# An image pipeline written slot by slot: the transposes of a quarter step change places, the mean is taken off in another form, and slots move

## The reference, cut to what matters

```
h = concat(cls_tok, (relu(x @ W0.T) * (x @ W1.T)) @ Wo.T)
def bitlinear(x, w):                       # mean and variance over tokens AND features
    x = (x - mean(x, (1, 2))) * rsqrt(var(x, (1, 2)) + 1e-5)
    return act_quant(x) @ weight_quant(w).T   # round(x * 127 / max|x| of a token)
q, k, v = bitlinear(ln(h), w_q), ..., ...  # 16 heads of 16
h += bitlinear(softmax(q @ k.T / 4) @ v, w_o)
x2 = ln(h); top2 of softmax(x2 @ gate_w)   # router
h += sum over the 2 experts of p_e * (silu(x2 @ g_e) * (x2 @ u_e)) @ d_e
```

## Time and profile before

| | |
|---|---|
| median of three executions | 2512.09 us (2507.2 to 2514.85) |
| profiled execution, its own time | 2501.11 us |
| its span | 2499.2 us |
| mean granted TensorE clock | 0.934 |
| TensorE (PE) busy | 2160.9 us, 86% |
| VectorE (DVE) busy | 1521.1 us, 61% |
| ScalarE (ACT) busy | 1203.2 us, 48% |
| GpSimd (POOL) busy | 965.7 us, 39% |

### The profile page before, as it was taken

How to read it: one execution, slowest core, us unless ns; L and a number is a source line. 1 busy time by engine, 2 the same in 40 slices (tenths; PEclk the granted TensorE clock), 3 DMA queues, 4 the chain that set the end, 5 groups by cost and what they waited for, 6 DMA issues and landing times. The chain is left out here.

```text
span 2499.2 us, 46805 instructions
## 1 busy us (share of the span) xinstructions
PE 2160.9 (86%) x12048; PEld 1071.8 (43%) x12049; DVE 1521.1 (61%) x4004; ACT 1203.2 (48%) x2360; POOL 965.7 (39%) x894
## 2 busy tenths in 40 slices
PE   4889989899898998988989888984069999999998
PEld 2433434443433433443344333322036666666665
DVE  3477877777766786777777778763453333333332
ACT  1256656455554565555555556551233444444443
POOL 2323343342333433344343343232335555555554
PEclk9899999999998998999999999886589999999999
DMA  2322232222222222222222122201433333333332
GB/s 96 80 81 61 72 90 69 73 69 82 78 67 67 69 81 70 79 63 77 74 77 81 52 82 79 75 10 34 152 85 56 54 55 53 54 54 53 54 53 39
DMA packets 181070, 171.96 MB, mean 69 GB/s; under 512 B 40002, under 2 KB 169620, under 8 KB 180884
## 3 DMA queue, kind: packets, MB, share of 16 engines
q1 hardware_dynamic: 150612, 134.94, 18.1%
q0 software_dynamic: 30272, 34.80, 8.9%
HBM read 100.82 MB, written 68.93 MB: 68 GB/s over the span
## 5 line engine op out<-in xcount | busy, mean ns | idle before, releaser
L1141 DVE TENSOR_REDUCE mxs<-bank 128x1 f32<-128x512 f32 x1024 | 698.0, 686 | 342.0 <-PE bank L491 272.0
L817 ACT ACTIVATE pt<-bank 128x512 f32<-128x512 f32 x1024 | 584.2, 593 | 369.7 <-PE bank L500 354.0
L491 PE MATMUL bank<-ks,qs 96*128 96x512 bf16 x1024 | 410.1, 401 | 74.5 <-DVE mxs L1141 53.0
L500 PE MATMUL bank<-qs,ks 99*128 99x512 bf16 x1024 | 405.7, 397 | 6.6 <-ACT pt L817 5.5
L1688 POOL DMA_INDIRECT out<-y_sb,ids x136 | 215.4, 1584 | 273.9 <-DMA out<-y_sb,ids 208.8
L509 PE MATMUL bank<-pt,v_sb 128*32 128x512 f32 x2048 | 288.6, 635 | 0.0
L491 PEld LDWEIGHTS bank<-ks,qs 96*128 96x128 bf16 x1024 | 104.7, 102 | 334.9 <-DVE mxs L1141 169.8
L985 POOL TENSOR_TENSOR cadd<-vcls,pr 128x256 f32<-128x256 f32 x64 | 40.5, 634 | 500.2 <-DVE pr L1188 498.5
L1813 DVE TENSOR_TENSOR hid_e<-bank,act_g 128x512 f32<-128x512 f32 x136 | 94.1, 692 | 211.8 <-PE bank L1734 211.8
L1817 DVE TENSOR_TENSOR hl<-bank,hh 128x512 bf16<-128x512 f32 x136 | 94.1, 692 | 211.2 <-ACT hh L1787 211.2
L1734 PE MATMUL bank<-gu_h,xh 128*128 x544 | 208.0, 382 | 12.6 <-issue 8.8
(11 more groups left out here) (281 smaller groups left out, 3499.8 us busy)
## 6 DMA issues: line engine op xcount, KB each, us to landing
qs<-qk_dram SPq DMA_DIRECT2D x128, 128.0 KB, 2.4
ks<-qk_dram SPq DMA_DIRECT2D x64, 192.0 KB, 3.1
xt<-x_t SPq DMA_DIRECT2D x16, 512.0 KB, 3.9
h_dram<-h_sb SPq DMA_DIRECT2D x16, 512.0 KB, 2.8
qs<-qk_dram SPq DMA_DIRECT2D x128, 64.0 KB, 2.1
ks<-qk_dram SPq DMA_DIRECT2D x64, 128.0 KB, 3.0
hw<-h_dram SPq DMA_DIRECT2D x16, 512.0 KB, 4.2
out<-hw SPq DMA_DIRECT2D x16, 512.0 KB, 2.9
```

Of the source, the lines that this page charges most:

```text
L491: mm(score[u % 2][:, :], qs[0:QK, h, blk(t)], ks[0:QK, h, :], start=True, stop=True) \
L500: mm(scoret[u % 2][:, :], ks[0:QK + MROWS, h, blk(t)], qs[0:QK + MROWS, h, :], start=True, stop=True).then_inc(s("pe_st"), 1)
L817: f(pt[:, t % 2, j, :], scoret[u % 2][:, :], ACT.Exp).then_inc(s("act_exp"), 1)
L1141: v.reduce_max(mxs[:, t, g * GH + j:g * GH + j + 1], score[u % 2][:, :], AX.X).then_inc(s("dve_mx"), 1)
```

## The change

TensorE's and the others' part in a quarter: `tg` moves from u = 7 to u = 6 and `mt` from u = 5 to u = 9, with ScalarE's copy from u = 6 to u = 10; `normalise` and `weigh` move from u = 8 and 9 to 7 and 8. The waits for bank d2 are changed to suit the new order. GpSimd's subtraction of the mean becomes an addition of the negated mean followed by a multiplication by 1.0, and VectorE computes the negated means (`nms1`, `nms2`). The rest is slot numbers: of the MLP, the router, the output's second half, layer norm statistics, the class row, the output's image statistics and the scatters. Comments at the ends of lines below are not in the diff.

```
-GATE_AT = (11, 15, 18, 35)
-UP_AT = (13, 17, 20, 37)
-HIDDEN_AT = (15, 19, 22, 39)
+GATE_AT = (11, 15, 18, 34)
+UP_AT = (13, 17, 20, 36)
+HIDDEN_AT = (14, 19, 22, 38)
 OUT_AT = (46, 49, 53, 57)
-STATS_AT = (52, 53, 60, 61)
-ROUTER_AT = (33, 34, 36, 38)
-SCATTER_AT = (48, 49, 50, 51, 52, 53, 54, 55)
+STATS_AT = (53, 54, 60, 61)
+ROUTER_AT = (34, 35, 37, 41)
+SCATTER_AT = (52, 53, 54, 55, 56, 57, 58, 59)
...                                   # TensorE
-                    if X.ok and at in (4, 6):
+                    if X.ok and at in (4, 5):
...
-                    if u == 5 and mt[0].ok:
-                        b, gg = mt
-                        wait(pe, s("dve_nm"), NG, b, gg + 1)
+                    if u == 6 and tg[0].ok:
+                        b, gg = tg
+                        wait(pe, s("act_pvs"), NG, b, gg + 1)
...
                         for t in range(TB):
+                            last = tr(d2[:, blk(t)], pvs[:, blk(t)], identf)
+                        last.then_inc(s("pe_tg"), 1)
+                    if u == 9 and mt[0].ok:
+                        b, gg = mt
+                        wait(pe, s("dve_nm"), NG, b, gg + 1)
+                        if tg[0].ok:
+                            wait(pe, s("dve_o"), NG, tg[0], tg[1] + 1)
+                        elif g == 1:
+                            wait(pe, s("dve_scs"), 1, C, 1)
+                        else:
+                            wait(pe, s("act_mt"), NG, C, gg)
+                        for t in range(TB):
                             last = tr(b16(d2)[0:MROWS * GH, blk(t)], nmp[:, t, :], id_bf[:, :])
                         last.then_inc(s("pe_mt"), 1)
...
-                    if X.ok and at in (27, 29):      # router's transposes
+                    if X.ok and at in (28, 30):
-                    if X.ok and at == 32:            # logits
+                    if X.ok and at == 33:
-                    if X.ok and at == 45:            # ranks
+                    if X.ok and at == 47:
-                    if W.ok and at == 34:            # class row's weighted sum, L734
+                    if W.ok and at == 35:
-                    if W.ok and at == 42:            # L744
+                    if W.ok and at == 44:
-                    if W.ok and at == 54:            # image sums, L753
+                    if W.ok and at == 51:
-                    if W.ok and at == 59:            # L759
+                    if W.ok and at == 56:
...                                   # ScalarE
-                    if u == 6 and mt[0].ok:
+                    if u == 10 and mt[0].ok:
-                    if C.ok and at == 25:            # exponential of the class row
+                    if C.ok and at == 27:
-                    if P.ok and at == 39:            # part_km
+                    if P.ok and at == 40:
...                                   # GpSimd
-                        g_.tensor_scalar(xn[:, :, :], xn[:, :, :], ms1[:, 0:1], None, ALU.subtract)
+                        g_.tensor_scalar(xn[:, :, :], xn[:, :, :], nms1[:, :], 1.0, ALU.add, ALU.mult)
-                    if W.ok and at == 56:
-                        g_.tensor_scalar(o_sb[:, W.par, :, :], o_sb[:, W.par, :, :], ms2[:, 0:1], None, ALU.subtract)
+                    if W.ok and at == 53:
+                        g_.tensor_scalar(o_sb[:, W.par, :, :], o_sb[:, W.par, :, :], nms2[:, :], 1.0, ALU.add, ALU.mult)
-                    if W.ok and at == 62:            # scales and rounding of the output
+                    if W.ok and at == 60:
...                                   # VectorE
-                    if u == 8 and tg[0].ok:
-                        normalise(*tg)
-                    if u == 9 and tg[0].ok:
+                    if u == 7 and tg[0].ok:
+                        normalise(*tg)
+                    if u == 8 and tg[0].ok:
                         weigh(*tg)
-                    if X.ok and at in (6, 7):        # output added to the residual
+                    if X.ok and at in (6, 9):
-                    if X.ok and at in (8, 11, 17):   # its layer norm statistics
+                    if X.ok and at in (10, 12, 15):
+                        v.scalar_tensor_tensor(nms1[:, :], red1[:, 0:1], -1.0 / total, cls_f[:, 0:1], ALU.mult, ALU.subtract)
-                    if P.ok and at in (14, 16):      # token maxima of the normed tokens
+                    if P.ok and at in (16, 17):
-                    if X.ok and at == 47:            # payload of the scatters
+                    if X.ok and at == 50:
-                    if W.ok and at in (46, 50):      # bn_stats of the attention output
+                    if W.ok and at in (43, 44):
-                    if W.ok and at == 44:            # class row normalised
+                    if W.ok and at == 46:
-                    if W.ok and at == 51:            # image moments
+                    if W.ok and at == 45:
-                    if W.ok and at == 52:
+                    if W.ok and at == 49:
-                    if W.ok and at == 55:
+                    if W.ok and at == 52:
+                        v.tensor_scalar(nms2[:, :], d0[:, 0:1], -1.0, None, ALU.mult)
-                    if W.ok and at in (58, 59):      # token maxima of the output
+                    if W.ok and at in (57, 58):
-                    if W.ok and at == 60:            # its scales
+                    if W.ok and at == 59:
```

More of the change, by code:

```diff
@@ L240, in token_phase @@
     ms1 = sb("ms1", [128, 2])
+    nms1 = sb("nms1", [128, 1])
     msq1 = sb("msq1", [128, 2])
@@ L295, in token_phase @@
     ms2 = sb("ms2", [128, 2])
+    nms2 = sb("nms2", [128, 1])
     msq2 = sb("msq2", [128, 2])
@@ L567, in body @@
                         if W.ok:
-                            wait(pe, s("dve_o"), NG, W, 1)
+                            wait(pe, s("act_mt"), NG, W, 3)
                         for c in range(DC):
@@ L632, in body @@
                         for t in range(TB):
+                            last = tr(d2[:, blk(t)], pvs[:, blk(t)], identf)
[6 more added lines that the diff above has]
+                        elif g == 1:
+                            wait(pe, s("dve_scs"), 1, C, 1)
+                        else:
+                            wait(pe, s("act_mt"), NG, C, gg)
+                        for t in range(TB):
                             last = tr(b16(d2)[0:MROWS * GH, blk(t)], nmp[:, t, :], id_bf[:, :])
                         last.then_inc(s("pe_mt"), 1)
-                    if u == 7 and tg[0].ok:
-                        b, gg = tg
-                        wait(pe, s("act_pvs"), NG, b, gg + 1)
-                        if mt[0].ok:
-                            wait(pe, s("act_mt"), NG, mt[0], mt[1] + 1)
-                        elif g == 1:
-                            wait(pe, s("dve_o"), NG, W, 2)
-                        else:
-                            wait(pe, s("dve_pvd"), 1, W, 1)
-                        for t in range(TB):
-                            last = tr(d2[:, blk(t)], pvs[:, blk(t)], identf)
-                        last.then_inc(s("pe_tg"), 1)
                     if P.ok and at == 10:
@@ L656, in body @@
                         if W.ok:
-                            wait(pe, s("dve_o"), NG, W, 2)
+                            wait(pe, s("act_mt"), NG, W, 4)
                         wait(pe, s("act_ct"), 1, C, 1)
@@ L703, in body @@
                             wait(pe, s("act_x2"), TB, X, TB)
-                            if W.ok:
+                            if C.ok:
+                                wait(pe, s("act_mt"), NG, C, 1)
+                            elif W.ok:
                                 wait(pe, s("dve_o"), NG, W, 3)
@@ L731, in body @@
                         else:
-                            wait(pe, s("dve_o"), NG, W, 3)
+                            wait(pe, s("act_mt"), NG, C, 1)
                         for t in range(TB):
@@ L739, in body @@
                         last.then_inc(s("pe_pvc"), 1)
-                    if W.ok and at == 42:
+                    if W.ok and at == 44:
                         wait(pe, s("dve_o"), NG, W, NG)
+                        if C.ok:
+                            wait(pe, s("act_mt"), NG, C, 2)
                         for k in range(NG):
@@ L994, in body @@
                     if P.ok and at == 12:
-                        hold(pool, s("dve_ms1"), 1, P, 1)
+                        hold(pool, s("dve_nms1"), 1, P, 1)
                         hold(pool, s("act_xh"), TB, P, TB)
-                        g_.tensor_scalar(xn[:, :, :], xn[:, :, :], ms1[:, 0:1], None, ALU.subtract).then_inc(s("pool_xm"), 1)
+                        g_.tensor_scalar(xn[:, :, :], xn[:, :, :], nms1[:, :], 1.0, ALU.add, ALU.mult).then_inc(s("pool_xm"), 1)
                         rsqrt(rs1[:, :], msq1[:, 1:2], 1, 128, "dve_ve", "pool_rs", P)
@@ L1384, in body @@
                             .then_inc(s("dve_qc"), 1)
-                    if C.ok and at == 22:
```

(7 more changed lines are left out.)

41 lines of the change are left out of this document (21 added, 20 removed).

## The result

The changed kernel takes 2419.09 us (median of 4 runs, 2412.62 to 2424.06), the kernel before 2509.64 on the same chip: 0.9636 of it, with an interval of 0.9605 to 0.9666.

What follows compares the result with a forecast made beforehand. No engine alone was taken as the bound: TensorE idles 8 to 11 us per step in several small waits. Terms summed to -3.7 a step, -37 over ten, -6 other steps, -1 end: -44, forecast 2468 us, range 2430 to 2513.

Steps and rivals of the forecast that it cites:

- the sign: Whole kernel: faster 0.75, the same 0.13, slower 0.12.
- the rivals' order: Three rivals: stall goes, clock holds, 2439 (0.16); VectorE and ScalarE take it back, 2503 (0.21); slower, 2535 (0.13).
- A: Rival: spaced scatters no longer stall TensorE and the clock holds, -6.2 us a step, 2439 in all; chance 0.16.
- item 6: TensorE's half clock behind the stall: part may not happen with less idle time, -0.6 us a step, 0 to -2.7.
- Item 3: Scatter stall near slot 55: 0.9 us won by reordering, 0.7 by spacing the scatters, -1.6 a step.
- Item 10: GpSimd's two-operation subtraction: 1.4 us instead of 2.85, from 1.05 to 1.92, hidden in a steady step.
- Items 1, 2, 4, 5, 8: Per-step terms; the first: first-quarter transposes of the maxima no longer wait for the class scores' copy, -0.5 us.
- item 8: VectorE in slots 40 to 46: more work moved in than is free, +0.6 us a step, 0 to +1.6.
- item 2: Third quarter: waits of L734, L744 and L784 covered by other matmuls, -1.2 us a step, at worst -0.3.
- Items 4 and 5: Step's end, maxima moved ahead of VectorE's bound, -0.9 us; slots 49 to 54, statistics leave, payload enters, -0.3.
- Item 7: ScalarE's copy moves ahead of exponentials that TensorE waits for: +0.5 us a step, at most +1.7.
- The other steps: Images 0 to 2 and 13 to 15, with little of the stall: -1 us each, -6 in all.

Runs made afterwards that it cites:

- e13: The changed kernel as it is, run again in another set: 2420.72 us, 0.9638 of the kernel before.
- e4: The kernel before without the token phase's scatters, a one-column fill in place of each: 2436.61 us, 0.9691 of the kernel before.
- e6: The changed kernel without the token phase's scatters, a one-column fill in place of each: 2391.53 us, 0.9557 of the kernel before.
- e2: The kernel before with only the two-operation form of both GpSimd subtractions: 2506.78 us, 0.9983 of the kernel before.
- e17: The kernel before with its row of scatters broken, four ahead of the mean's subtraction and four behind: 2479.70 us, 0.9919 of the kernel before.
- e14: The changed kernel with the old quarter order and the one-operation form, so only the slots moved: 2489.63 us, 0.9912 of the kernel before.
- e9: The changed kernel with the old order within a quarter: 2452.52 us, 0.9995 of the kernel before, which took 2454.26 in that set.
- e10: The changed kernel with the one-operation form in both subtractions: 2446.64 us, 0.9960 of the kernel before, which took 2454.26 in that set.

## Why the prediction was wrong

Right in the sign, in the rivals' order (A was nearest: the stall did go) and in the duration of the new form; the time was wrong by 49 us, the saving by 46 (90 against 44). About half of the 46 is in the ten steps (58 against 37), half outside them. The step that failed in a steady step is item 6, "The clock. [...] -0.6, from 0 to -2.7": it measured -3.8 (-3.1 in e13's trace). It took the one stretch of half clock that the rows showed (6 us behind slot 55; 5.5 a step on the mean, of 10.6) for all of it, and let a third to two thirds of the idle time decide. But the clock column of the earlier trace rows stood there for whole steps: 0.96 and 0.94 are about 10 us of half clock a step, worth 5. With 5 as that item's end and half of it taken, the sum of a step is -5.6, next to the -5.8 measured; that would be luck in part, for the idle terms were too large by 1.5.

- *Item 3*, the stall of the scatters, -1.6: the whole 2.65 went, its best end. The scatters cost 2.35 of idle and 1.1 by the clock in a steady step before (e4), and nothing after (e6). "What is spaced seems mostly covered" was the right reading, priced too low.
- *Item 10*, the form: the duration was right, 1.12 us against 1.4 taken and 1.05 to 1.92 allowed, but "hidden" was wrong. It is worth 24 to 33 us in the changed slots. GpSimd was busy for 36% of the steady steps before, but in the changed slots TensorE waits for the end of its chain (L588), which the earlier trace rows did not show. On the kernel before it was indeed nothing (e2).
- *Items 1, 2, 4, 5, 8*, idle time: L734, L744 and L784 went from 22.2 to 7.1 in all, 0.9 a step and not 1.2. The maxima's transposes rose from 8.3 to 19.6 where a fall was forecast. The third quarter rose by 0.74 as a whole (waits for maxima in slot 43, 1.6 us), so item 8's loss was larger than item 2's gain. Items 4 and 5 did not show: TensorE's idle time in slots 61 to 63 went from 2.4 to 2.7, in slots 50 to 52 from 1.0 to 0.9. The first two quarters gave 0.3 and 1.0, the last 5.3. Net idle: -1.6 against the -3.1 that the items other than the clock sum to. Their size was too hopeful; the clock more than made it up.
- *Item 7*, ScalarE, +0.5: 0.2 at most, for over the kernel the wait of L500 (now L502) for exponentials rose from 5.5 to 8.7; the second quarter, where most of it was placed, fell by 0.95.
- *The other steps*, -7 with the end: measured -29, some 22 us of the miss. Images 2 and 13 alone gave 5.6 and 8.8. They have the scatters, too, and before idled 2.9 and 2.3 us for them in slots 55 to 58, in waits of at most 1.5, which "little of the stall" left out; image 13's step also had 10.2 of half clock before and none after.

The Trainium skill, TensorE: Matmul & The Clock Gate, Part 1, ties the clock to how busy the engine has recently been. The traces agree in part: half clock began inside or just behind waits of 2.65 (slot 55), 2.81 (slot 1) and 4.25 us (the back edge), but in e17 also in slot 34, behind waits of 0.79 (slot 29) and 0.40 (slot 34), in six of ten steps, and behind the same waits in one of ten before. By the rule of the Trainium skill, GPSIMD Engine Reference, section 3.1, one and two operations would cost the same: the two-operation form at 1.12 us is near the 0.9 estimated from it, the one-operation form at 2.86 (e14's subtraction) is not; the measurement decides.

## What to carry to other kernels

Write down, before any wait, what the granted clock costs over whole steps (time times one less the clock, from rows by stretch): it is a term of its own, it may be larger than all idle time an edit removes, and it may only move when one wait goes: breaking the row alone gave 21 us (e17, by its trace next to none of it in the steady steps), the order on top of the moved slots 45. Price a set of small edits together and in the slots that they will have, not one by one on the old kernel: order and form gave 0 there, each alone, and 69 us here, in part because the new slots bring in waiting that they remove. An engine that is busy for a third of the time can still be the last link from one step to the next; follow its last result to its first reader before calling a cut hidden.

## What was not expected of the hardware

- Behind eight scatters in a row from GpSimd, TensorE's results reach VectorE and ScalarE late (TensorE then idles 2.7 us in a step; the scatters cost 3.6 with the clock). Split by other work they cost a steady step nothing. With the loop written out the row costs 2.45 of idle time, in shorter waits and almost without half clock.
- The loop's back edge leaves TensorE idle for 1.5 to 2.4 us a lap before, 2.4 to 4.4 in the two traces of the changed kernel and 2.7 to 5.3 in e17, and half clock at it; with the steps written out the changed kernel is 28 us shorter and the kernel before 46. What sets the length was not tested.
- A subtraction of one operand on GpSimd, f32 to f32, takes 2.85 us for 1024 elements, and 1.12 as add and multiply by one.
- The kernel before took 2500.7 to 2510.6 in five sets of runs and 2454.3 in one, at a granted clock of 0.93 and 0.94; e9's and e10's edits took the same time in a set of either kind. No trace of it from the set at 2454.3 exists, so the cause stays open.
